# Moving five single-bank steps to the first slot of their groups and two layer-norm moments to the end of theirs, in an attention and feed-forward kernel

## What is computed

```python
h = x @ W1 + b1                        # (16, 512, 384), split per head in q, k, v of width 8
w = einsum('bhqd,bhkd->bhqk', q, k) / sqrt(8)
w = softmax(causal(w))                 # 16 x 16 x 512 x 512
a = einsum('bhqk,bhkd->bhqd', w, v)
x = layernorm(x + a @ Wp + bp)

x_prev = shift_by_one_token(x)
xr = mu_r * x + (1 - mu_r) * x_prev
xk = mu_k * x + (1 - mu_k) * x_prev
r = sigmoid(xr @ W_r.T)
out = r * (square(relu(xk @ W_k.T)) @ W_v.T)
x = layernorm(x + out)
```

## Time and profile before

| | |
|---|---|
| median of 3 runs | 703.65 us (703.49 to 703.93) |
| the profiled execution | 706.27 us, span 704.5 us |
| mean granted TensorE clock | 0.944 |
| TensorE matmul | 599.4 us busy, 85% of the span |
| VectorE | 548.2 us, 78% |
| ScalarE | 448.1 us, 64% |
| GpSimd | 415.3 us, 59% |
| chain that ended last | TensorE 69%, VectorE 20%, ScalarE 5%, issue 3%, DMA 2%, GpSimd 1% |

### The profile page before, as it was taken

One profiled execution on the slowest core, in us unless ns is written; L12 is line 12 of the kernel. 1 busy time (PEld: TensorE's weight loads), 2 busy tenths in 40 slices (PEclk: granted clock), 3 DMA queues, 4 the chain that ended last, 5 costly groups with the idle time before them and its releaser, 6 DMA issues.

```text
span 704.5 us, 17539 instructions
## 1 busy us (share of the span) xinstructions
PE 599.4 (85%) x6662; PEld 266.4 (38%) x6662; DVE 548.2 (78%) x1651; ACT 448.1 (64%) x854; POOL 415.3 (59%) x548
## 2 busy tenths in 40 slices
PE   2558898898989899998989899998989899998863
PEld 1113333344343434344343434344443434343442
DVE  1585878788888888888898888888888888885437
ACT  2104776776767676776767676776767676667831
POOL 4102335666657585766657484767657584848573
PEclk8555999999999999999999999999999999999977
DMA  5542535343334525353334426353434426201100
GB/s 175 87 137 47 153 62 154 62 142 66 116 78 92 138 48 153 76 154 77 123 65 105 124 47 167 62 153 78 128 75 119 94 49 166 48 10 26 33 16 30
DMA packets 65194, 65.79 MB, mean 93 GB/s; under 512 B 8725, under 2 KB 54870, under 8 KB 65110
## 3 DMA queue, kind: packets, MB, share of 16 engines
q1 hardware_dynamic: 64546, 64.21, 37.1%
q10 hardware_dynamic: 564, 0.46, 0.3%
HBM read 34.70 MB, written 29.88 MB: 92 GB/s over the span
## 4 chain that ended last, share of the span: by engine, by line
PE 69%; DVE 20%; ACT 5%; issue 3%; DMA 2%; POOL 1%; POOLq 0%; SPq 0%; DVEq 0%; ACTq 0%
PE ops L608 19%; PE sps L581 13%; DVE rowmax L813 12%; PE tps L543 10%; PE spare L473 9%; PE spare L487 5%; PE sps L566 5%; ACT probs L741 4%; PE spare L518 2%; DVE stats L819 2%; PE spare L502 1%; DVE y L852 1%; PE spare L507 1%; PE spare L515 1%; DVE attn L846 1%
## 5 line engine op out<-in xcount | busy, mean ns | idle before, releaser
L813 DVE TENSOR_REDUCE rowmax<-sps 128x1 f32<-128x512 f32 (+7 forms) x1024 | 401.1, 448 | 89.4 <-PE sps L581 88.4
L741 ACT ACTIVATE probs<-tps 128x512 f32<-128x512 f32 x640 | 347.2, 597 | 137.1 <-PE tps L543 137.0
L993 POOL TENSOR_SCALAR_AFFINE_SELECT probs<-probs 128x512 f32<-128x512 f32 x256 | 158.2, 635 | 226.8 <-ACT probs L741 226.8
L608 PE MATMUL ops<-probs,vop 128*32 128x384 f32 (+3 forms) x2048 | 173.4, 445 | 3.4 <-POOL probs L993 2.5
L543 PE MATMUL tps<-qop,kop 50*128 50x384 bf16 (+3 forms) x1024 | 126.3, 305 | 36.1 <-ACT probs L741 34.1
L581 PE MATMUL sps<-kop,qop 48*64 48x512 bf16 (+7 forms) x2048 | 130.2, 309 | 12.8 <-DMA kop<-d_parts 12.8
L566 PE MATMUL sps<-qmask,dup 64*128 64x128 bf16 (+1 forms) x640 | 70.0, 215 | 34.7 <-DVE rowmax L813 27.8
L543 PEld LDWEIGHTS tps<-qop,kop 50*128 50x128 bf16 x1024 | 34.2, 94 | 151.8 <-ACT probs L741 77.2
L608 PEld LDWEIGHTS ops<-probs,vop 128*32 128x32 f32 x2048 | 50.5, 109 | 84.3 <-issue 67.0
L566 PEld LDWEIGHTS sps<-qmask,dup 64*128 64x128 bf16 x640 | 31.3, 94 | 85.9 <-DVE rowmax L813 82.0
L581 PEld LDWEIGHTS sps<-kop,qop 48*64 48x64 bf16 x2048 | 43.1, 106 | 51.0 <-issue 15.5
(11 more groups left out here) (113 smaller groups left out, 541.3 us busy)
## 6 DMA issues: line engine op xcount, KB each, us to landing
qop<-d_parts SPq DMA_DIRECT2D x64, 192.0 KB, 4.0
kop<-d_parts SPq DMA_DIRECT2D x63, 192.0 KB, 4.4
d_parts<-qk_parts SPq DMA_DIRECT2D x15, 768.0 KB, 3.9
d_parts<-qk_parts SPq DMA_DIRECT2D x15, 512.0 KB, 4.8
d_parts<-qk_parts SPq DMA_DIRECT2D x17, 256.0 KB, 4.7
xT<-x_by_channel SPq DMA_DIRECT2D x16, 256.0 KB, 2.7
xres<-x SPq DMA_DIRECT2D x16, 256.0 KB, 3.1
out<-result SPq DMA_DIRECT2D x15, 256.0 KB, 2.5
```

The costliest lines, as they stand in the source:

```text
L608: last = nc.tensor.matmul(ops[32 * t:32 * t + 32, BLK * a:SEQ], vop[:, par, a, QUARTET * half + t, hh, :], probs[:, g % 2, i, off:off + w] ...
L741: nc.scalar.activation(probs[:, g % 2, i, :], tps[:, bank(n), :], ACT.Exp, scale=SCALE)\
L813: last = nc.vector.reduce_max(rowmax[:, par, QUARTET * half + i, a:a + 1], sps[:, bank(n), off:off + w], axis=AX_X)
L993: last = nc.gpsimd.affine_select(out=v, in_=v, compare_op=ALU.is_ge, fill=0.0, base=0, pattern=[[0, QUARTET], [1, BLK]], channel_multiplie ...
```

## The change

Five uses go from the second slot (1) of their group to the first (0): q, value, hT, sums of half 0, v. As every engine reads its order from the same table, their readers on ScalarE and VectorE move too, ahead of exponentials 2 and 3 and of maxima 2 and 3. Y's and z's moments go from between the maxima to behind the group's last maxima and its second use.

```diff
 SPARE_USES = {
-    ("A", "q"): (0, 1), ("A", "k"): (1, 1),
-    ("S", "v"): (9, 1), ("S", "max0"): (5, 1),
-    ("T", "max1"): (1, 0), ("T", "sums0"): (8, 1),
-    ("D", "sums1"): (2, 0), ("D", "attnT"): (3, 0), ("D", "project"): (4, 0), ("D", "hT"): (7, 1),
-    ("E", "key"): (3, 1), ("E", "gate"): (5, 0), ("E", "value"): (6, 1),
+    ("A", "q"): (0, 0), ("A", "k"): (1, 1),
+    ("S", "v"): (9, 0), ("S", "max0"): (5, 1),
+    ("T", "max1"): (1, 0), ("T", "sums0"): (8, 0),
+    ("D", "sums1"): (2, 0), ("D", "attnT"): (3, 0), ("D", "project"): (4, 0), ("D", "hT"): (7, 0),
+    ("E", "key"): (3, 1), ("E", "gate"): (5, 0), ("E", "value"): (6, 0),
 }
...
                     for _, use, n in ORDER[b, g, 0]:
                         spare_use(use, n)
-                    if tg == 4 and active("D", tb) and before("D", tb) < LAST:
-                        n = before("D", tb)
-                        is_read(dve, "project", n)
-                        layer_norm_moments(y, 0, n, stats_done, moments_done)
...
-                    if tg == 9 and active("E", tb) and before("E", tb) < LAST - 1:
-                        n = before("E", tb)
-                        wait(dve, z_done, n + 1)
-                        layer_norm_moments(z, 1, n, stats2_done, moments2_done)
                     if active("S", b):
                         reduce_chunk(before("S", b), g, 2)
                         reduce_chunk(before("S", b), g, 3)
                     for _, use, n in ORDER[b, g, 1]:
                         spare_use(use, n)
+                    if tg == 4 and active("D", tb) and before("D", tb) < LAST:
+                        n = before("D", tb)
+                        is_read(dve, "project", n)
+                        layer_norm_moments(y, 0, n, stats_done, moments_done)
+                    if tg == 9 and active("E", tb) and before("E", tb) < LAST - 1:
+                        n = before("E", tb)
+                        wait(dve, z_done, n + 1)
+                        layer_norm_moments(z, 1, n, stats2_done, moments2_done)
```

## The result

The changed kernel takes 680.68 us (median of 4 runs, 680.11 to 682.05) against 703.79 us of the kernel before on the same chip; the ratio is 0.9669, with a 95% interval of 0.9647 to 0.9692. The forecast was 681.9 us within 674 to 694. The profiled execution of the changed kernel is 682.05 us with a span of 680.3.

The account below looks back on a forecast made before the run. Neither TensorE (85% busy) nor VectorE (78%) alone was the limit; handshake holes gain 3.77 us per frame, less 0.40, 0.50, 1.03 and 0.37, walked to 1.44; 21.8 over the run from 703.65 gives 681.9 us, range 674 to 694.

Parts of the forecast that it names:

- The holes: TensorE's handshake waits in first slots: hT and sums0 gain 0.59 each, value 0.68, q 0.62, v 0.56 us per frame.
- q, taken back 0.40: Groups 0 and 1: q's VectorE step delays the maxima behind it, so group 1's first mask comes 0.40 us late.
- sums0, taken back 0.50: Groups 8 and 9: reciprocal and multiplies ahead of the maxima delay the next group's mask by 0.34 plus 0.16 us.
- Y's moments and the meeting, taken back 1.03: Groups 4 to 6: GpSimd's earlier causal mask stretches group 5's result pair by 0.41; group 6's mask comes 1.03 us late.
- Group 6 at VectorE's pace, 3.92 from mask to mask: Group 6: VectorE's queue sets the time between first masks at 3.92 us, of which 0.37 is wait.
- Z's moments at 0: Groups 9 to 1: moving z's moments behind the last maxima costs a steady frame 0 us.
- Rule and rows: Group 5: by the skill's VectorE-GpSimd exclusion, result's second instruction waits out the mask, some 0.2 us more per frame, 684 us.
- Sum over the run: All frames: eleven steady ones gain 1.44 us each, 15.8; with the other frames and the tail, 21.8 us.
- The last frame and the tail: End of the run: ScalarE paces T and GpSimd the tail; gain 0.5 us, bounded by 0 and 1.5.
- GpSimd's chain starts perhaps 0.5 earlier: Tail after the last frame: the GpSimd chain that paces it starts sooner, giving the 0.5 us gain there.
- rival 3: Groups 7 to 0: GpSimd's queue makes PV wait for a late causal mask; slower, 709 us if held 2.8 us; chance 0.06.

Follow-up runs that it names:

- the first experiment: Changed kernel with the second half of result moved from group 5 to group 3, behind the first half: frame 36.84 us, 670.68 us, ratio 0.9525 to the kernel before.

## Why the prediction was right, point by point

- **The holes** held as read. Hidden hT and sums0: group 8 falls by 0.58, and hT back costs 0.59, the very size. Undone alone, q and value give back less than the hole's size, since the wait that their reader caused goes with them. For v it is 0.42 instead of 0.56: the 0.14 is the exponential's handshake, which the late first mask of group 9 hides without v.
- **q, taken back 0.40**: 0.31. The chain was right; the maximum starts 0.67 after q's step, not 0.75, because VectorE's next instruction starts some 0.08 before an end, which I had used elsewhere and not here. Groups 0 and 1 gain 0.32, not 0.22.
- **sums0, taken back 0.50**: 0.50 (316.23 is 0.73 after its group's T at 315.50, instead of 0.23). Groups 8 and 9 gain 0.61; the terms of the sum give 0.65 (0.59 + 0.56 - 0.50).
- **Y's moments and the meeting, taken back 1.03**: the first mask of group 6 came 1.15 after its T (342.11 to 343.26), 0.92 late. The causal mask met the pair as forecast and stretched it by 0.35 instead of 0.41. The forecast had taken the pair's end as 0.80 after the mask's start, from the earlier trace rows, where the mask takes 0.72; here it takes 0.63. Rstd did not slip by 0.05: the moments ended at 4.40 after group 4's T instead of 4.53, before GpSimd was free.
- **Group 6 at VectorE's pace, 3.92 from mask to mask**: 3.86 (305.57 to 309.43 in the frame before). Groups 4 to 7 together gain 0.78; 0.60 was forecast.
- **Z's moments at 0**: 0.01.
- **Rule and rows**: the pair ends 0.08 to 0.09 after the mask's end in the changed kernel (342.61 against 342.52), and so does the h pair of the earlier trace rows (663.35 against 663.27). The second instruction of the pair, which starts 0.02 after the mask, takes 0.69 instead of 0.34; the first, already under way, is not stretched. So VectorE does wait out the whole mask. In all fourteen profiles, each instruction of such a pair that starts with more than 0.26 us of a causal mask to come (122 of them) ends 0.08 to 0.09 after that mask's end. The Trainium skill (SBUF — State Buffer, "Who interferes with whom") says that of a VectorE instruction in a two-port mode and a GpSimd instruction whoever issues first has the shared port pair for the whole instruction, and the other fully blocks; for the mask this case's traces agree. What was wrong is the price that the prediction put on the rule, 0.2 more per frame: the held instruction ends 0.08 behind the mask and does not run its 0.34 after it, so the stretch is 0.35 and not more than 0.41. For rstd the rule does not hold: its 1.05 us on four columns held nothing.
- **Sum over the run**: a frame gains 1.71 (1.44 forecast), so eleven frames bring 18.8 instead of 15.8. Frame 2 gains 2.64, not 1.86: I had taken the meeting out of it, but not the 0.52 that the missing pair itself leaves; its 36.76 is nearly the frame of the first experiment. Frame 1 gains 1.37 (1.55), frame 0 0.94 (0.84), frame 14 1.25 (1.22). That frame 0 agrees is partly luck: it takes 35.31 to 38.45 us in the profiles here, with how late in it TensorE's matmuls come to full speed. K's matmul in its group 1 takes 2.07 us in the kernel before and 2.08 in the changed one, but 1.12 in the kernel with y's moments back and the result pair gone, whose frame 0 takes 35.31.
- **The last frame and the tail were wrong in sign**: +0.5 forecast, -0.9 measured (61.07 us from frame 15's start to the end instead of 60.19). The step that failed is "GpSimd's chain starts perhaps 0.5 earlier". The slack that rival 3 named is used up in this one frame, whose groups are short because S is gone: v in the first slot made group 9's causal mask late, the mask of group 0 came after two scaled products, and PV waited. The experiment with v alone back shows it: there PV does not wait for the mask, and groups 1 and 2 of frame 15 take 3.23 and 2.46 as in the kernel before. Changed kernel, timeline of frame 15's group 1:

```profile
624.25 1.28 PE L608 MATMUL ops<-probs,vop 128*32 128x512 f32 x8 [1.02 <-POOL probs L993]
```

Its windows ahead of that PV and from it on:

```profile
621.00:624.00 3.00, 1.70 (x25) 0.52 (x17) 0.00 (x0) 2.70 (x7) 2.92 (x3) 1.00 0.01 3
624.00:628.50 4.50, 4.25 (x24) 1.51 (x28) 1.30 (x6) 2.74 (x6) 4.15 (x8) 0.62 0.03 6
```

TensorE waited 1.02, and behind the wait its granted clock fell to a mean of 0.62, so groups 1 and 2 took 3.77 and 3.49 instead of 3.23 and 2.46. With z's moments or the result pair moved, groups 1 and 2 of this frame take 3.56 and 2.56: the wait for the mask stays, the clock does not fall. So the wait costs about 0.4 and the clock about 1.1.

In sum, 21.8 were forecast, and the spans differ by 24.2, the medians by 23.1. The total is closer than its parts: the steady frames gained 3.0 more than forecast and frame 2 0.8 more, and the last frame and the tail took 1.4 back.

## What to carry to other kernels

Find the holes that handshakes leave between two steps of the bound engine, and put independent work of that engine there; then walk the queue of the engine that reads the result, since what it must read now stands ahead of what the bound engine waits for next. A move is worth what ends last after it: the same edit gave -0.18 or +0.67 us per frame, depending on one pair of instructions two steps away. When a group starts earlier, look for what another engine starts earlier with it, for here a GpSimd mask moved into VectorE's normalisation.

## What the runs showed of the hardware

- TensorE's granted clock can fall in the middle of dense work (5.47 us busy of 6.00). With value back, it fell behind the waits of 0.76 and 0.53 in frames 3, 6, 10 and 13, but not in the seven others like them; each time it cost about 1.56 us per frame, four times what moving value is worth. In the changed kernel it fell behind the wait of 1.02 in frame 15; with z's moments back the same wait is there (1.03), and the clock stayed at 1.00. What decides it is open.
- The recorded clock can be wrong at the start of a run. In the changed kernel it reads 1.00 where q's matmul takes 2.07 us, against 1.13 at full clock in steady frames; in the kernel before, the same stretch reads 0.50 and q takes as long. Changed kernel, timeline:

```profile
22.86 2.07 PE L487 MATMUL spare<-xT,w1p 128*128 128x512 f32 x2
```

And the window around it:

```profile
20.00:30.00 10.00, 5.44 (x33) 1.86 (x34) 4.95 (x10) 0.69 (x1) 0.00 (x0) 1.00 0.79 120
```

  So the mean of 0.979 of this run against 0.944 before says nothing of its speed.
- VectorE's normalising instruction (TENSOR_SCALAR, 128 columns) that meets a GpSimd causal mask over 512 columns ends 0.08 to 0.09 us after the mask, if more than 0.26 of the mask is still to come (the pair takes 0.95 instead of 0.60 here, 0.92 in the earlier trace rows). GpSimd's sum over 512 columns does the same near the end (0.34 to 0.65 us); its rstd instruction of 1.05 us over four columns does nothing to it.
